# A hand-written order of every engine up to the third step of a software-pipelined attention and feed-forward kernel on one Trainium2 core

## The chip, the core and the metric

The kernel runs on one core of one Trainium2 chip. The metric is the device time of one execution in microseconds (us), lower is better. Five engines work side by side, each through its own list of instructions in order: PE (TensorE, matrix products), DVE (VectorE), ACT (ScalarE), POOL (GpSimd) and SP (SyncE, which here issues nearly all DMA transfers). They meet only at semaphores. An instruction that waits for a semaphore holds back everything behind it on its own engine.

## What is computed

The reference, cut to what matters (x is 32 x 128 x 1024, ctx is 32 x 128 x 256, the projections are 128 x 128, the dequantised weight is 1024 x 1024):

```python
def attend(up, down, Wq, Wk, Wv, Wskip):      # per batch element
    q, k, v = Wq @ up, Wk @ down, Wv @ down
    attention = softmax(q.T @ k / sqrt(128))  # 1024 x 256
    return Wskip @ up + (attention @ v.T).T
w = (unpacked_nibbles(qweight) - round(zeros / scales).T) * scales.T
x = x + attend(layernorm(x), ctx, Wq, Wk, Wv, Wskip)
x = x + layernorm(x) @ w + bias
```

## The kernel before

One batch element (a tile of 128 rows by 1024 columns) is one unit of work, and there are 32 of them. Below, f(b, j) is the function f for element b (from 0), part j. The pipeline is laid out over steps t: in step t the element b = t has its attention scores and probabilities made, n = t + 1 its first layernorm finished and its keys and values made, m = t + 2 its first statistics, a = t - 1 its attention output, residual and second layernorm, q = t - 2 its feed-forward product, and c = t - 3 its last output written. Each engine has a function step(t) with the order of its work in a step, and before it a function run_in() with a hand-written order for the first steps. In the kernel before, run_in covers steps 0 and 1 on every engine, and run_steps(step, 2) does the rest. There is no planner: the order on each engine is the order in the source, and the semaphores only hold an instruction back.

The work of one element, by engine, with the lines by which the profile knows it:

- PE. scores(b, j), j = 0 to 3: six products each into one of two banks (L891); the first needs keys_lo(b) of DVE, j = 0 and j = 2 need centred_lo(b, 0) and (b, 1) of POOL, j = 2 and 3 need exps(b, 0) and (b, 1) of ACT, and j = 0 and 1 need exps(b-1, 2) and (b-1, 3). keys_values(n) (L900, L902, L904) needs values_lo(n-1) and context_max(n) of DVE. skip_attend(a, h), h = 0, 1 (L917, L921), needs the transposed probabilities of the half, h. ffn(q, h) (L926, and L930 for ffn_terms, which adds bias and zero points out of seed_w): 17 products a half, from the transposed normalised rows xnt_hi and xnt_lo and the weight wf.
- DVE. stats1, aggregate1, variance1 (L594, L602, L608) for the first layernorm; value_scale(n) (L619 to L627), whose last instruction waits for inverse_std1(n) of POOL; keys_lo, values_lo (L645, L650, L652); row_max (L657); invert(b, j) (L662), the reciprocal of a row sum, after exps(b, j); probs_lo(b, h) (L666); residual(a, h) (L676); stats2, aggregate2 (L681 to L691); scale_product (L700); context_max (L614).
- ACT. centre, centred_hi (L433, L440), keys_hi, values_hi (L461 to L470), exps (L478), probs_hi(b, h) (L487), which needs two normalise of POOL, apply_norm2 and xn_high (L496, L505).
- POOL. normalise(b, j) (L255, two instructions), which waits for invert(b, j); inverse_std1(m) (L263); centred_lo(n, h) (L270); inverse_std2(a) (L277, L279); split_row_sum(a) (L289 to L295); xn_low(a) (L300, two instructions); write_out(c, h) (L249).
- SP. turn_probs(b, h): two DMA transposes, of the high and the low part of the probabilities; turn_xn(a): two DMA transposes, of xn_high and xn_low; loads of x and ctx; stores.

Some work is done once and lies within the run-in and step 2: nibbles(k) on DVE (L719, L720), k = 0 to 3, unpacks a quarter of the weight, and unpack(k) on ACT (L509, L510) turns it into wf, from which the first ffn(0, 0) waits quarter by quarter. zero_point_quotient, zero_point_remainder, zero_point_rounding and seed_sources on POOL (L315 to L358) are chains of small instructions, each of which waits for the one before; PE transposes their result (turn_seed_rows, L875) into bank y0, and DVE copies it to seed_w (seed_rows, L730). In the kernel before, ffn(0, 0) waits for seed_rows before it starts, since it writes the same bank y0.

Of the kernel before, what the change touches and what calls it, by code (L numbers as in the profile page):

```python
# [15 lines left out]
def xattn_ffn_program(nc, x, ctx_in, wq, wk, wv, wskip, qweight, scales, zeros, bias, out):  # L16
# [26 lines left out]
    with es:  # L43
# [100 lines left out]
        def _(sp):  # L144
# [84 lines left out]
        def _(pool):  # L229
# [106 lines left out]
            def zero_point_rounding():  # L336
# [24 lines left out]
            def run_in():  # L361
# [16 lines left out]
                inverse_std1(3)  # L378
# [35 lines left out]
            run_steps(step, 2)  # L414

        @block.scalar
        def _(act):
# [95 lines left out]
            def run_in():  # L513
# [22 lines left out]
                probs_hi(1, 0)  # L536
                exps(1, 3)
                unpack(1)
                keys_hi(2)
                values_hi(2)  # L540
                probs_hi(1, 1)
                apply_norm2(0)
                xn_high(0)

            def step(t):
# [11 lines left out]
                if t == 2:  # L557
                    unpack(2)
# [3 lines left out]
                if t == 2:  # L562
                    unpack(3)
# [10 lines left out]
            run_steps(step, 2)  # L574

        @block.vector
        def _(dve):
# [149 lines left out]
            def seed_rows():  # L727
# [69 lines left out]
            def step(t):
# [9 lines left out]
                if t == 2:  # L807
                    nibbles(3)
# [13 lines left out]
                if t == 2:  # L822
                    seed_rows()
# [29 lines left out]
            run_steps(step, 2)  # L853

        @block.tensor
        def _(pe):
# [109 lines left out]
            def run_in():  # L966
# [14 lines left out]
                skip_attend(0, 1)  # L981

            def step(t):
# [7 lines left out]
                if t == 2:  # L991
                    turn_seed_rows()
# [14 lines left out]
            run_steps(step, 2)  # L1007
# [24 lines left out]
```

## Time and profile before

| what | value |
|---|---|
| runs | 525.06, 525.08, 527.37 us (median 525.08) |
| the profiled execution | 525.56 us |
| its span in the trace | 523.6 us |
| busy share PE, DVE, ACT, POOL | 95%, 82%, 71%, 90% |
| chain that ended last | PE 82%, POOL 7%, DVE 4%, DMA 3%, ACT 2% |
| mean granted TensorE clock | 0.993 |

The profiled execution took 525.56 us, of which the trace spans 523.6. Times of instructions below are microseconds from the start of the span. Engines overlap, so the shares don't add up. The clock is given as a share of full speed (2.4 GHz is 1.00, 1.2 GHz is 0.50).

### The profile page before, as it was taken

To read this page: it belongs to the slowest core of one execution; us is meant where nothing else is said; L and a number is where in the kernel's file an instruction comes from. 1 tells how busy PE (TensorE), PEld (TensorE's weight loads), DVE (VectorE), ACT (ScalarE), POOL (GpSimd) and SP (SyncE) were. 2 spreads that over 40 slices of the span, in tenths; PEclk is the share of its full clock that TensorE was granted. 3 is DMA by queue.
4 is the path that set the end of the run, shared out by engine and by line. 5 is a ranking of instruction groups with operands and counts; after the bars stand their busy time and mean duration, and the time that the engine had idled before them with its cause. 6 is when DMAs were issued, how large, how long until landed. Compare 5 with 4: busy or idle time off the path is not lost.

```text
span 523.6 us, 9244 instructions
## 1 busy us (share of the span) xinstructions
PE 496.0 (95%) x2668; PEld 301.3 (58%) x2668; DVE 427.9 (82%) x981; ACT 373.0 (71%) x844; POOL 471.2 (90%) x717
## 2 busy tenths in 40 slices
PE   4638999999999999999999999999999999999996
PEld 3525565566666555666656566655656666565642
DVE  5899788889888888988888898888889888887752
ACT  3978877777877777787777778777776877777520
POOL 4899899999999999999999999999999999999753
PEclk9989999999999999999999999999999999999999
DMA  7537787797897789689788878988797799757753
GB/s 295 181 75 144 150 200 194 181 203 171 182 173 201 177 185 202 176 175 190 186 181 185 194 180 172 188 195 179 177 195 185 167 188 196 176 131 141 164 124 123
DMA packets 227059, 92.65 MB, mean 177 GB/s; under 512 B 209472, under 2 KB 214080, under 8 KB 227008
## 3 DMA queue, kind: packets, MB, share of 16 engines
q1 hardware_dynamic: 226288, 91.91, 77.4%
q8 instruction: 21, 0.34, 0.3%
q14 instruction: 30, 0.25, 0.2%
q10 hardware_dynamic: 720, 0.14, 0.1%
HBM read 23.87 MB, written 16.78 MB: 78 GB/s over the span
## 4 chain that ended last, share of the span: by engine, by line
PE 82%; POOL 7%; DVE 4%; DMA 3%; ACT 2%; issue 2%; SPq 1%; POOLq 0%; ACTq 0%
PE ps_y L926 39%; PE ps_e L891 15%; PE ps_o L921 13%; PE ps_o L917 7%; PE ps_kv L902 3%; PE ps_y L930 2%; PE ps_kv L904 2%; POOL sb_prob L255 2%; DMA sb_xnt_lo<-sb_xn_lo 1%; DMA sb_wskip<-in_L_xattn_Wskip_dram 1%; POOL sb_xc_lo L270 1%; ACT sb_prob L478 1%; POOL sb_xn_lo L300 1%; DVE sb_neg_max L657 1%; DVE sb_st L594 0%
## 5 line engine op out<-in xcount | busy, mean ns | idle before, releaser
L926 PE MATMUL ps_y<-sb_wf,sb_xnt_hi 128*128 128x512 f16 x512 | 191.9, 380 | 2.9 <-DMA sb_xnt_lo<-sb_xn_lo 1.8
L926 PE MATMUL ps_y<-sb_wf,sb_xnt_lo 128*128 128x512 f16 x512 | 191.8, 379 | 0.0
L478 ACT ACTIVATE sb_prob<-ps_e,sb_neg_max 128x256 f32<-128x256 f32 x256 | 118.5, 471 | 58.3 <-DVE sb_neg_max L657 58.3
L255 POOL TENSOR_SCALAR sb_prob<-sb_prob,sb_rsum 128x256 f32<-128x256 f32 x256 | 123.0, 494 | 14.9 <-DVE sb_rsum L662 14.8
L666 DVE TENSOR_TENSOR sb_p_lo<-sb_prob,sb_p_hi 128x1024 f16<-128x1024 f32 x64 | 78.1, 1220 | 49.2 <-ACT sb_p_hi L487 49.2
L891 PE MATMUL ps_e<-sb_k_hi,sb_xc_hi 128*128 128x256 f32 x256 | 90.2, 353 | 8.1 <-DVE sb_k_lo L645 5.6
L926 PEld LDWEIGHTS ps_y<-sb_wf,sb_xnt_hi 128*128 128x128 f16 x512 | 49.9, 98 | 62.5 <-DMA sb_xnt_lo<-sb_xn_lo 2.8
L249 POOL TENSOR_TENSOR sb_o<-sb_prod,sb_x 128x512 f32<-128x512 f32 x63 | 80.4, 1276 | 5.6 <-DVE sb_prod L700 5.5
L657 DVE TENSOR_REDUCE sb_neg_max<-ps_e 128x2 f32<-128x512 f32 x128 | 84.7, 681 | 0.4
L926 PEld LDWEIGHTS ps_y<-sb_wf,sb_xnt_lo 128*128 128x128 f16 x512 | 50.1, 98 | 56.6
L487 ACT ACTIVATE sb_p_hi<-sb_prob 128x1024 f16<-128x1024 f32 x64 | 67.3, 1052 | 18.5 <-issue 15.5
L270 POOL TENSOR_TENSOR sb_xc_lo<-sb_xc,sb_xc_hi 128x512 fp32r<-128x512 f32 x62 | 80.1, 1292 | 0.2 <-ACT sb_xc_hi L440 0.2
L496 ACT ACTIVATE sb_xn<-sb_x,sb_nb,sb_rstd 128x1024 f32<-128x1024 f32 x32 | 43.0, 1343 | 51.6 <-POOL sb_nb L279 51.6
L891 PE MATMUL ps_e<-sb_k_lo,sb_xc_hi 128*128 128x256 f32 x256 | 72.9, 285 | 0.0
L891 PE MATMUL ps_e<-sb_k_hi,sb_xc_lo 128*128 128x256 f32 x256 | 72.6, 284 | 0.0
L300 POOL TENSOR_TENSOR sb_xn_lo<-sb_xn,sb_xn_hi 128x512 f16<-128x512 f32 x63 | 72.5, 1172 | 0.1
L891 PEld LDWEIGHTS ps_e<-sb_k_hi,sb_xc_hi 128*128 128x128 f32 x256 | 49.2, 192 | 20.3 <-DVE sb_k_lo L645 6.5
L700 DVE TENSOR_TENSOR sb_prod<-ps_y,sb_scale_row 128x512 f32<-128x512 f32 x64 | 43.8, 684 | 12.9 <-PE ps_y L930 12.4
L478 ACT ACTIVATION_READ_ACCUMULATOR sb_prob<-ps_e,sb_neg_max 128x1 f32 x256 | 51.1, 200 | 0.0
L891 PEld LDWEIGHTS ps_e<-sb_k_lo,sb_xc_hi 128*128 128x128 f32 x256 | 49.4, 193 | 2.3
L676 DVE SCALAR_TENSOR_TENSOR sb_x<-ps_o,sb_o_scale,sb_x 128x512 f32<-128x512 f32 x64 | 47.2, 738 | 3.7 <-PE ps_o L921 3.7
L921 PE MATMUL ps_o<-sb_pt_hi,sb_v_hi 128*128 128x512 f16 x128 | 49.2, 384 | 0.5 <-DMA sb_pt_lo<-sb_p_lo 0.4
(123 smaller groups left out, 925.2 us busy)
## 6 DMA issues: line engine op xcount, KB each, us to landing
sb_x<-in_x_dram SPq DMA_DIRECT2D x32, 512.0 KB, 4.0
out_dram<-sb_o SPq DMA_DIRECT2D x64, 256.0 KB, 2.4
sb_ctx<-in_ctx_dram SPq DMA_DIRECT2D x32, 128.0 KB, 2.7
sb_q<-in_L_ffn_qweight_dram SPq DMA_DIRECT2D x4, 512.0 KB, 9.0
sb_pt_hi<-sb_p_hi SPq DMA_TRANSPOSE x64, 3.0
sb_pt_lo<-sb_p_lo SPq DMA_TRANSPOSE x64, 2.8
sb_scale_row<-in_L_ffn_scales_dram SPq DMA_DIRECT2D x1, 512.0 KB, 10.3
sb_xnt_hi<-sb_xn_hi SPq DMA_TRANSPOSE x32, 2.8
```

The source lines that it names most:

```text
L249: pool.tensor_tensor(o_sb[:, c % 2, cols], prod[:, h, :], x1[:, c % 3, cols], ALU.add).then_inc(out_done[h], 1)
L255: last = pool.tensor_scalar(prob[:, j, t, :], prob[:, j, t, :], rsum[:, j, t:t + 1], P_SCALE, ALU.mult, ALU.mult)
L270: pool.tensor_tensor(xc_lo[:, n % 3, cols], xc[:, cols], xc_hi[:, n % 3, cols].bitcast(F32), ALU.subtract).then_inc(xclo_done, 1)
L300: last = pool.tensor_tensor(xn_lo[:, k:k + KT // 2, :], xn[:, k:k + KT // 2, :], xn_hi[:, k:k + KT // 2, :], ALU.subtract)
L478: done = act.activation(prob[:, j, t, :], ps_e[j % 2][:, t, :], ACT.Exp, bias=neg_max[:, j, t:t + 1], accum_out=esum[:, j, t:t + 1])
L487: act.activation(p_hi[:, h, :, :].rearrange("n k (t m) -> n k t m", m=P), prob[:, 2 * h:2 * h + 2, :, :].rearrange("n j t (k m) -> n k (j ...
L657: dve.tensor_reduce(neg_max[:, j, :], ps_e[j % 2][:, :, :], AX.X, ALU.max, negate=True).then_inc(max_done[j], 1)
L666: dve.tensor_tensor(p_lo[:, h, :, :].rearrange("n k (t m) -> n k t m", m=P), prob[:, 2 * h:2 * h + 2, :, :].rearrange("n j t (k m) -> n k ...
L676: dve.scalar_tensor_tensor(x1[:, a % 3, cols], ps_o[h][:, :], o_scale[:, a % 3:a % 3 + 1], x_sb[:, a % 4, cols], ALU.mult, ALU.add).then_i ...
L891: last = pe.matmul(ps_e[j % 2][:, t, :], xc_p[s][:, b % 3, cols], k_p[m][:, b % 2, :], start=i == 0, stop=i == 2)
L921: last = pe.matmul(ps_o[h][:, :], v_p[s][:, a % 3, k * P:(k + 1) * P], pt_p[m][:, h, k, :], start=False, stop=k == MT - 1 and i == 2)
L926: pe.matmul(ps_y[h][:, :], xnt_p[s][:, q % 2, kt, :], wf[:, kt, h * HALF:(h + 1) * HALF], start=kt == 0 and s == 0, stop=False)
```

## The change

Run_in is extended on PE, DVE, ACT and POOL so that it covers step 2 as well, and run_steps begins with step 3 there; on SP run_in is reordered and run_steps still begins with step 2. What differs in order:

- DVE: after row_max(1, 3) stands value_scale(2), and keys_lo(2) comes ahead of nibbles(1), probs_lo(1, 0) and the statistics stats1(3), aggregate1(3), variance1(3); row_max(2, 0) comes ahead of probs_lo(1, 1). In what was step 2, nibbles(3) and seed_rows stand after row_max(2, 2); stats1(4), aggregate1(4), variance1(4), and invert(2, 2) with them, come after residual(1, 1), row_max(2, 3), stats2(1, 1) and aggregate2(1). keys_lo(n) waits for values_hi(n) for every n from 2 on.
- POOL: zero_point_rounding is cut after its sixth instruction, and its last four (zero_point_sign) come after inverse_std2(0); split_row_sum(0) and xn_low(0) come ahead of seed_sources; inverse_std1(3) comes after normalise(2, 0), behind seed_sources; inverse_std1(4) comes after normalise(2, 3).
- ACT: probs_hi(1, 0) comes after values_hi(2); unpack(1) after xn_high(0); unpack(2) ahead of centre(3); unpack(3) after exps(2, 2); exps(2, 3) ahead of probs_hi(2, 0).
- PE: keeps the order of step 2, but turn_seed_rows comes after skip_attend(1, 1) and writes bank y1, and ffn(0, 0) waits for seed_rows only before its last product.
- SP: turn_xn is cut in two; load_ctx(4) comes ahead of turn_probs(1, 0), and the high transpose of turn_xn(0) ahead of turn_probs(1, 1).

```diff
@@ SP
-            def turn_xn(a):
+            def turn_xn_hi(a):
...
+            def turn_xn_lo(a):
...
                 sp.wait_ge(kv_done, 2)
                 load_ctx(3)
-                turn_probs(1, 0)
                 sp.wait_ge(kv_done, 3)
                 load_ctx(4)
+                turn_probs(1, 0)
                 sp.wait_ge(x1_done[1], 1)
                 load_x(4)
+                turn_xn_hi(0)
                 turn_probs(1, 1)
-                turn_xn(0)
+                turn_xn_lo(0)
@@ POOL
                 zero_point_rounding()
-                inverse_std1(3)
                 normalise(1, 2)
                 normalise(1, 3)
                 inverse_std2(0)
-                seed_sources()
+                zero_point_sign()
                 split_row_sum(0)
                 xn_low(0)
+                seed_sources()
+                normalise(2, 0)
+                inverse_std1(3)
+                normalise(2, 1)
+                normalise(2, 2)
+                centred_lo(3, 0)
+                inverse_std2(1)
+                centred_lo(3, 1)
+                normalise(2, 3)
+                inverse_std1(4)
+                write_out(0, 0)
+                split_row_sum(1)
+                xn_low(1)
@@ ACT
                 exps(1, 2)
-                probs_hi(1, 0)
                 exps(1, 3)
-                unpack(1)
                 keys_hi(2)
                 values_hi(2)
+                probs_hi(1, 0)
                 probs_hi(1, 1)
                 apply_norm2(0)
                 xn_high(0)
+                unpack(1)
+                exps(2, 0)
+                unpack(2)
+                centre(3)
+                exps(2, 1)
+                keys_hi(3)
+                values_hi(3)
+                exps(2, 2)
+                unpack(3)
+                centred_hi(3)
+                exps(2, 3)
+                probs_hi(2, 0)
+                apply_norm2(1)
+                probs_hi(2, 1)
+                xn_high(1)
@@ DVE
             def keys_lo(n):
                 src = (ps_o[1], ps_y[0], ps_kv)[min(n, 2)]
-                if n == 2:
-                    dve.wait_ge(kvhi_done, 3)
+                if n >= 2:
+                    dve.wait_ge(kvhi_done, n + 1)
...
                 row_max(1, 3)
+                value_scale(2)
                 stats2(0, 0)
+                invert(1, 2)
+                residual(0, 1)
+                invert(1, 3)
+                stats2(0, 1)
+                aggregate2(0)
+                keys_lo(2)
                 nibbles(1)
-                invert(1, 2)
+                probs_lo(1, 0)
+                values_lo(2)
+                row_max(2, 0)
+                probs_lo(1, 1)
+                context_max(3)
+                nibbles(2)
                 stats1(3, 0)
                 stats1(3, 1)
                 aggregate1(3)
                 variance1(3)
-                value_scale(2)
-                residual(0, 1)
-                probs_lo(1, 0)
-                invert(1, 3)
-                stats2(0, 1)
-                aggregate2(0)
-                keys_lo(2)
-                values_lo(2)
-                context_max(3)
-                nibbles(2)
-                probs_lo(1, 1)
+                invert(2, 0)
+                residual(1, 0)
+                row_max(2, 1)
+                value_scale(3)
+                row_max(2, 2)
+                nibbles(3)
+                seed_rows()
+                invert(2, 1)
+                keys_lo(3)
+                values_lo(3)
+                stats2(1, 0)
+                residual(1, 1)
+                row_max(2, 3)
+                stats2(1, 1)
+                aggregate2(1)
+                invert(2, 2)
+                stats1(4, 0)
+                stats1(4, 1)
+                aggregate1(4)
+                invert(2, 3)
+                variance1(4)
+                probs_lo(2, 0)
+                context_max(4)
+                scale_product(0, 0)
+                probs_lo(2, 1)
@@ PE
             def ffn_terms(q, h):
+                if q == 0:
+                    pe.wait_ge(rows_done, 1)
...
             def ffn_ready(q, h):
                 if ran(q, 1):
                     pe.wait_ge(prod_done[h], q)
-                else:
+                elif h == 1:
                     pe.wait_ge(rows_done, 1)
...
+                scores(2, 0)
+                keys_values(3)
+                skip_attend(1, 0)
+                scores(2, 1)
+                scores(2, 2)
+                skip_attend(1, 1)
+                turn_seed_rows()
+                scores(2, 3)
+                ffn(0, 0)
+                ffn(0, 1)
```

The bank of turn_seed_rows and of the copy in seed_rows is `ps_y[1]` after the change, `ps_y[0]` before. The lines `if t == 2:` with their calls are gone from the four functions step(t).

## Rows read from the trace of the kernel before

**Rows 1.** Stretches: us; busy (count) of PE, PEld, DVE, ACT, POOL; clock; DMA share; GB/s

```profile
35.00:40.00 5.00, 2.27 (x9) 2.09 (x10) 4.93 (x13) 2.50 (x4) 4.89 (x8) 0.50 0.47 123
...
110.00:125.00 15.00, 15.00 (x83) 9.30 (x83) 12.77 (x31) 11.16 (x27) 14.16 (x21) 1.00 0.82 200
```

**Rows 2.** Waits of PE from 0 to 75 us: us in total, times, longest

```profile
PE ps_e L891 <- DVE sb_k_lo L645: 5.6, 2, 5.4
...
PE ps_y L926 <- DMA sb_xnt_lo<-sb_xn_lo: 1.1, 1, 1.1
PE ps_y L926 <- ACT sb_wf L510: 1.0, 1, 1.0
```

**Rows 3.** Busy time from 54 us on, columns as in rows 1

```profile
54.00:60.00 6.00, 6.00 (x34) 3.50 (x33) 4.33 (x7) 4.95 (x9) 4.68 (x7) 1.00 0.62 129
60.00:500.00 440.00, 439.87 (x2395) 267.57 (x2394) 371.95 (x853) 325.65 (x748) 413.82 (x607) 1.00 0.82 180
```

**Rows 4.** Timeline of PE: start, duration (us), engine, line, what [idle before it]

```profile
31.97 0.38 PE L921 MATMUL ps_o<-sb_pt_hi,sb_v_lo 128*128 128x512 f16 x1
37.73 0.58 PE L891 MATMUL ps_e<-sb_k_hi,sb_xc_hi 128*128 128x256 f32 x1 [5.38 <-DVE sb_k_lo L645]
...
39.18 0.23 PE L900 MATMUL ps_m<-sb_amax,sb_ones 128*128 128x1 bf16 x1
...
43.01 0.38 PE L921 MATMUL ps_o<-sb_pt_hi,sb_v_lo 128*128 128x512 f16 x1
...
49.98 0.39 PE L926 MATMUL ps_y<-sb_wf,sb_xnt_hi 128*128 128x512 f16 x1 [1.08 <-DMA sb_xnt_lo<-sb_xn_lo]
...
58.31 0.47 PE L891 MATMUL ps_e<-sb_k_hi,sb_xc_hi 128*128 128x256 f32 x1
...
66.40 0.39 PE L926 MATMUL ps_y<-sb_wf,sb_xnt_hi 128*128 128x512 f16 x1
```

**Rows 5.** Timeline of DVE

```profile
27.52 1.13 DVE L650 SCALAR_TENSOR_TENSOR sb_wsk_lo<-sb_proj,sb_sk_scale,sb_wsk_hi 128x128 fp32r<-128x128 f32 x1
...
30.76 0.71 DVE L719 TENSOR_SCALAR sb_nib<-sb_q 128x1024 int32<-128x1024 int32 x1
...
32.06 1.26 DVE L594 BATCH_NORM_STATS2 sb_st<-sb_x 128x6 f32<-128x512 f32 x2
...
34.95 1.22 DVE L666 TENSOR_TENSOR sb_p_lo<-sb_prob,sb_p_hi 128x1024 f16<-128x1024 f32 x1
...
37.19 0.48 DVE L645 SCALAR_TENSOR_TENSOR sb_k_lo<-ps_kv,sb_rstd,sb_k_hi 128x256 fp32r<-128x256 f32 x1
...
46.92 1.20 DVE L730 COPY sb_seed_w<-ps_y 16x1024 bf16<-16x1024 bf16 x1
...
52.58 0.15 DVE L691 TENSOR_SCALAR sb_ve<-sb_mv 128x1 f32<-128x1 f32 x1
```

**Rows 6.** Timeline of POOL

```profile
30.66 0.26 POOL L338 TENSOR_SCALAR sb_zp<-sb_zp 128x8 f32<-128x8 f32 x1
31.01 1.10 POOL L339 TENSOR_SCALAR sb_zp<-sb_zp 128x8 f32<-128x8 f32 x1
32.19 0.20 POOL L340 TENSOR_TENSOR sb_zp<-sb_zp 128x8 f32<-128x8 f32 x1
...
46.99 0.94 POOL L255 TENSOR_SCALAR sb_prob<-sb_prob,sb_rsum 128x256 f32<-128x256 f32 x2
47.89 0.57 POOL L263 TENSOR_TENSOR sb_rstd<-sb_ve,sb_neg_half 128x1 f32<-128x1 f32 x1
...
54.89 1.83 POOL L255 TENSOR_SCALAR sb_prob<-sb_prob,sb_rsum 128x256 f32<-128x256 f32 x2 [1.15 <-DVE sb_rsum L662]
56.92 1.27 POOL L249 TENSOR_TENSOR sb_o<-sb_prod,sb_x 128x512 f32<-128x512 f32 x1 [0.21 <-DVE sb_prod L700]
...
60.07 2.28 POOL L300 TENSOR_TENSOR sb_xn_lo<-sb_xn,sb_xn_hi 128x512 f16<-128x512 f32 x2
```

**Rows 7.** PE by stretch: us, busy (instructions), granted clock, DMA share, GB/s

```profile
34.50:35.00 0.50, 0.00 (x0) 0.52 0.00 0
41.00:41.50 0.50, 0.50 (x4) 0.65 2.82 277
```

More of the change, by code:

```diff
@@ L181, in turn_xn @@
                     last_hi_loaded if a == B - 1 else xnt_loaded[par], 16)
+            def turn_xn_lo(a):
+                par = a % 2
                 sp.wait_ge(rs_done, a + 1)
@@ L204, in step @@
                 if ran(a):
-                    turn_xn(a)
+                    turn_xn_hi(a)
+                    turn_xn_lo(a)
             def run_in():
@@ L343, in zero_point_rounding, with zero_point_sign @@
                 link(pool.tensor_scalar(size, size, ROUND, None, ALU.subtract))
+            def zero_point_sign():
+                size, sign, small = zp(WORK), zp(WORK + 1), zp(TMP)
                 link(pool.tensor_tensor(size, size, sign, ALU.mult))
@@ L413, in _ @@
             run_in()
-            run_steps(step, 2)
+            run_steps(step, 3)
         @block.scalar
@@ L556, in step @@
                     exps(b, 1)
-                if t == 2:
-                    unpack(2)
                 if ran(b):
@@ L561, in step @@
                     probs_hi(b, 0)
-                if t == 2:
-                    unpack(3)
                 if ran(b):
@@ L573, in _ @@
             run_in()
-            run_steps(step, 2)
+            run_steps(step, 3)
         @block.vector
@@ L730, in seed_rows @@
                 dve.tensor_copy(seed_w[0:ROWS, :].rearrange("m (p t) -> m p t", t=ZT),
-                                ps_y[0][0:ROWS, :].bitcast(BF16).rearrange("m (t p) -> m p t", p=P)).then_inc(rows_done, 1)
+                                ps_y[1][0:ROWS, :].bitcast(BF16).rearrange("m (t p) -> m p t", p=P)).then_inc(rows_done, 1)
             def run_in():
@@ L806, in step @@
                     value_scale(n)
-                if t == 2:
-                    nibbles(3)
                 if ran(m):
@@ L821, in step @@
                     row_max(b, 2)
-                if t == 2:
-                    seed_rows()
                 if ran(a):
@@ L852, in _ @@
             run_in()
-            run_steps(step, 2)
+            run_steps(step, 3)
         @block.tensor
@@ L874, in turn_seed_rows @@
                 for t in range(ZT):
-                    last = pe.transpose(ps_y[0][0:ROWS, :].bitcast(BF16)[:, t * P:(t + 1) * P], seed_src[:, t, :],
+                    last = pe.transpose(ps_y[1][0:ROWS, :].bitcast(BF16)[:, t * P:(t + 1) * P], seed_src[:, t, :],
                                         ident16[:, :])
@@ L990, in step @@
                     skip_attend(a, 0)
-                if t == 2:
-                    turn_seed_rows()
                 if ran(b):
@@ L1006, in _ @@
             run_in()
-            run_steps(step, 2)
+            run_steps(step, 3)
 _INS = ["x", "ctx_1024", "L0_xattn_Wq", "L0_xattn_Wk", "L0_xattn_Wv", "L0_xattn_Wskip",
```

## The prediction

> **What bounds the kernel now.** I read busy time by stretch first, then the waits, then the timelines of the first 80 us. From step 3 on the only limit is PE: 15.00 of 15.00 us busy, with POOL close behind at 14.16 [rows 1]. From 54 to 500 us PE was busy in 445.87 of 446 us [rows 3]. What lies in front of that is ragged: between 35 and 40 us PE was busy 2.27 of 5 us at half its clock [rows 1], because scores(2, 0) waited 5.4 us for keys_lo(2); later ffn(0, 0) waited 1.1 us for the transposed xn_low(0) and 1.0 us for the weight [rows 2]. So the change is worth what it moves the first moment from which PE no longer waits. I measure that at the start of ffn(1, 0), at 66.40 us before, with scores(3, 0) at 58.31 as the mark ahead of it [rows 4]. PE's work behind that is the same and full, so a shift there is a shift of the end.
>
> **Step 1: scores(2, 0), a gain of 3.0 us.** keys_lo(2) started at 37.19. Taken from in front of it are nibbles(1), stats1(3) with its two small ones and probs_lo(1, 0): slots of 1.2, 1.6 and 1.1 us by start-to-start, 3.9 in all [rows 5]. What stays then meets two waits: 0.2 us for keys_values(2), and 0.7 for the end of skip_attend(0, 1) at 32.35 [rows 4]. 37.2 - 3.9 + 0.9 = 34.2, and scores(2, 0) at 34.7, not 37.73.
>
> **Step 2: most of it is lost at keys_values(3).** It needs context_max(3), which now stands behind nibbles(1) 1.2, probs_lo(1, 0) 1.1, values_lo(2) 0.8, row_max(2, 0) 0.6 and probs_lo(1, 1) 1.1. 34.6 + 4.8 = 39.4, plus 0.5 for itself: 39.9 against 39.18 before [rows 4]. PE idles from 36.1. The clock had fallen to half at 34.5 and came back at about 41.3, some 3.6 us after PE resumed [rows 4, 7]; resuming at 39.9 I let it come back at 43.5, so keys_values(3) and skip_attend(1, 0) take 4.8 us, to 44.8 (before: to 43.4). Then scores(2, 1) and (2, 2), 1.4 us, and skip_attend(1, 1), 2.0, to 48.2 us; turn_seed_rows 0.5; scores(2, 3); ffn(0, 0) at 49.4. xn_low(0) is ready at 43.4 (step 3), so that wait of 1.1 us is gone. unpack(3) is done at 51.3, just ahead of the seventh pair at 52.0. The two ffn(0, h) took 58.31 - 49.98 less the 1.0 us wait, 7.35 [rows 2, 4]: PE is free at 56.8 us. If nothing else held, that would be 1.5 us gained.
>
> **Step 3: POOL reaches inverse_std1(3) late.** Between 30.66 and 47.89 POOL never idled: ten links of rounding, inverse_std1(3), three normalise, inverse_std2(0), seed_sources, split_row_sum(0), xn_low(0) [rows 6]. The new order does exactly these before the first standard deviation of element 3 is ready. The sum depends on holds: L339 took 1.10 us beside nibbles(1), its neighbour of the same size 0.20 [rows 5, 6], and the same is seen beside probs_lo. Four such holds stay (nibbles 1 and 2, both probs_lo), one, beside nibbles(3), goes, 0.8 us. 30.7 + 17.2 - 0.8 gives 47.1; I take 47.3. xn_low(0), now ahead of seed_sources, ends at 43.4 and not 47.0.
>
> By the Trainium skill (GPSIMD Engine Reference, Specifications) POOL's SBUF interfaces contend with Vector instructions that have two SBUF inputs, and the first of values_lo is one. If it held POOL too, its two calls would add about 0.6 us. The trace has the reverse there: L650 took 1.13 us while POOL's centred_lo ran on [rows 5], so I add nothing.
>
> **Step 4: DVE waits behind it.** value_scale(3) ends with an instruction that needs inverse_std1(3). Before, that was long done. Now DVE has run everything up to there by about 46.7 and waits to 47.3. Queued behind are row_max(2, 2), nibbles(3) and seed_rows, and only then invert(2, 1), for which POOL's normalise(2, 1) waits. 47.5 + 0.6 + 1.2 = 49.3 for seed_rows. From seed_rows to the end of aggregate2(1) the old trace shows 46.92 to 52.73, 5.8 us [rows 5], and it holds just what the new order puts ahead of invert(2, 2). So invert(2, 1) comes at 50.5 and invert(2, 2) at 55.1 (before: 50.30).
>
> **Step 5: POOL idles twice and is late for the rest.** From 46.99 to 62.35 POOL did normalise(2, 0) to xn_low(1): 15.4 us, of which 1.15 and 0.21 idle and 0.9 the first normalise, so 13.1 us of work, holds included [rows 6]. The new list has the same 13.1 us from normalise(2, 1) on. It starts at 50.6, stops from 51.5 to 55.1 for invert(2, 2), and ends at 50.6 + 13.1 + 3.6 = 67.3 us, 4.9 later than before.
>
> **Step 6: what PE sees.** The transpose of xn_low(0) let PE start 3.0 us after POOL was done (47.0 to 49.98) [rows 4, 6]. 67.3 + 3.0 = 70.3 for ffn(1, 0), 3.9 us after the 66.40 of before. A second chain ends close by: normalise(2, 3) is done at 61.5, probs_hi(2, 1) takes 1.0, probs_lo(2, 1) ends at 64.4 after waiting for POOL's write_out, and row_max(3, 0) stands behind it. The old probs_lo(2, 1) ended 7.1 us ahead of ffn(1, 0); keeping that whole gives 71.5, +5.1, but some of it was PE's own pace. Between 3.9 and 5.1 I take 4.3, nearer the first, whose terms are all durations. In step 4 POOL's next xn_low is ready at about 82, its transpose at 85, ffn(2, 0) due at 86: nothing is added, nothing recovered, since PE is full. The SP and ACT moves cost nothing: the transposes of element 1 land by 45 us and are read at 46.2; exps(2, 3) is done by 54.8 while POOL is what probs_hi waits for.
>
> Sum: 525.56 + 4.3 = 529.9 for a profiled execution like this one; the median of the runs is 0.5 below it, so **529.4 us**. 0.5% (2.6 us) is about what a measurement here can tell from no change.
>
> **Rivals.**
>
> *The early gain stays (faster).* The place is xn_low(1) on POOL. PE free at 56.8 is worth 1.5 us, 523.5 in all, if xn_low(1) is done by 56.8 + 8.1 - 3.0 = 61.9 us. For it: PE's own path through step 2 has no new wait, and a clock that stayed up would add up to 0.8. Against it: it needs POOL 5.4 us earlier than I have it, and with no wait on DVE at all invert(2, 2) comes at about 51, so xn_low(1) at 64. It would take holds on POOL much shorter than the traces show. A gain over 2.6 us is 0.05, one up to there 0.05.
>
> *The delay is smaller (within 0.5%).* The holds overlap more, inverse_std1(3) is ready at 46, DVE hardly waits, POOL's second stop is 2 us: ffn(1, 0) at 68, +1.6, 526.7. Chance 0.14.
>
> *The clock falls again.* On the forecast PE idles about 4 us between scores(3, 1) and scores(3, 2), waiting for exps(3, 0). Before, 2.2 us without work from 32.35 was followed by half clock at 34.5, which lasted until 41.3 [rows 4, 7]. A fall here puts scores(3, 2), skip_attend(2, 1) and scores(3, 3), 3.4 us at full speed, partly at half: +1 to +2 us, 530.4 to 531.4. The Trainium skill (TensorE: Matmul & The Clock Gate, What's actually happening) says that the throttled state is the default and activity lifts it, so a busier start would keep the clock and a new hole lose it. Chance 0.26.
>
> The forecast itself, +2.6 to +5.2, has 0.50. In all: slower 0.76, within 0.5% 0.19, faster 0.05. The range is 526.2 to 531.6: from the smaller delay to the clock case.
>
> **What would show it.** Right: scores(2, 0) at 34.7; keys_values(3) near 40; the last instruction of value_scale(3) waiting for L263 near 47; POOL idle twice for 3 us before L255, put down to invert; xn_low(1) ending near 67; waits of PE before scores(3, 2) and ffn(1, 0); 15.25 us steps from there. Wrong: L263 of element 3 ready before 45, or POOL without those stops, or PE that catches up later.

## The result and the profile after

The changed kernel took 530.62 us (median of 5 runs, 529.74 to 531.53) against 525.09 us for the kernel before in the same runs: ratio 1.0105, 95% interval [1.0092, 1.0119], 5.5 us slower. The forecast was 529.4 us. The profiled execution took 530.62 us, its span is 528.7 us (before: 525.56 and 523.6).

Three views of the changed kernel answer to the rows of before. First its waits, of PE from 0 to 80 us, then of POOL and DVE from 28 to 75 us (us in total, times, longest). Lines have moved: L943 is scores, L952 the first product of keys_values, L973 the attention, L978 the feed-forward product, L260 normalise, L268 inverse_std1, L275 centred_lo, L282 inverse_std2, L305 xn_low, L498 exps, L507 probs_hi, L644 context_max, L657 the last instruction of value_scale, L675 keys_lo, L692 invert, L696 probs_lo, L706 residual, L721 the last of aggregate2.

```profile
PE ps_e L943 <- ACT sb_prob L498: 4.5, 3, 3.2
PE ps_m L952 <- DVE sb_amax L644: 4.1, 1, 4.1
PE ps_e L943 <- DVE sb_k_lo L675: 2.7, 2, 2.4
...
POOL sb_prob L260 <- DVE sb_rsum L692: 6.5, 2, 3.4
...
DVE sb_x L706 <- PE ps_o L973: 2.7, 2, 2.1
DVE sb_sk_scale L657 <- POOL sb_rstd L268: 0.9, 1, 0.9
```

The wait for keys_lo(2), 5.4 us long before [rows 2, 4], is 2.4 us. In its place PE waits 4.1 us for context_max(3), and 3.2 us for exps(3, 0). POOL, which never idled at this point before, waits 6.5 us in two stops for invert.

The timelines of PE, DVE and POOL, in this order (start, duration, engine, line, what, [idle before it]):

```profile
34.46 0.39 PE L943 MATMUL ps_e<-sb_k_hi,sb_xc_hi 128*128 128x256 f32 x1 [2.42 <-DVE sb_k_lo L675]
...
39.56 0.16 PE L952 MATMUL ps_m<-sb_amax,sb_ones 128*128 128x1 bf16 x1 [4.12 <-DVE sb_amax L644]
...
56.71 0.36 PE L943 MATMUL ps_e<-sb_k_hi,sb_xc_hi 128*128 128x256 f32 x1
...
65.87 0.36 PE L943 MATMUL ps_e<-sb_k_hi,sb_xc_hi 128*128 128x256 f32 x1 [3.21 <-ACT sb_prob L498]
...
68.09 0.63 PE L973 MATMUL ps_o<-sb_pt_lo,sb_v_hi 128*128 128x512 f16 x1
...
71.04 0.39 PE L978 MATMUL ps_y<-sb_wf,sb_xnt_hi 128*128 128x512 f16 x1
```

```profile
47.09 0.21 DVE L657 TENSOR_SCALAR sb_sk_scale<-sb_v_scale,sb_rstd 128x1 f32<-128x1 f32 x1 [0.89 <-POOL sb_rstd L268]
...
50.15 0.14 DVE L692 RECIPROCAL sb_rsum<-sb_esum 128x2 f32<-128x2 f32 x1
...
54.20 0.15 DVE L692 RECIPROCAL sb_rsum<-sb_esum 128x2 f32<-128x2 f32 x1
...
61.80 1.67 DVE L696 TENSOR_TENSOR sb_p_lo<-sb_prob,sb_p_hi 128x1024 f16<-128x1024 f32 x1 [3.18 <-ACT sb_p_hi L507]
```

```profile
46.41 0.57 POOL L268 TENSOR_TENSOR sb_rstd<-sb_ve,sb_neg_half 128x1 f32<-128x1 f32 x1
50.39 0.96 POOL L260 TENSOR_SCALAR sb_prob<-sb_prob,sb_rsum 128x256 f32<-128x256 f32 x2 [3.41 <-DVE sb_rsum L692]
54.45 0.94 POOL L260 TENSOR_SCALAR sb_prob<-sb_prob,sb_rsum 128x256 f32<-128x256 f32 x2 [3.09 <-DVE sb_rsum L692]
...
64.27 2.27 POOL L305 TENSOR_TENSOR sb_xn_lo<-sb_xn,sb_xn_hi 128x512 f16<-128x512 f32 x2
```

And PE by stretches (us, busy (instructions), granted clock, DMA share, GB/s):

```profile
34.00:35.00 1.00, 0.54 (x4) 1.00 0.58 134
35.00:36.00 1.00, 0.43 (x4) 1.00 0.58 128
36.00:38.00 2.00, 0.00 (x0) 0.57 0.01 3
...
67.00:68.00 1.00, 1.00 (x4) 0.50 0.28 64
68.00:69.00 1.00, 1.00 (x4) 0.50 1.29 114
69.00:70.00 1.00, 1.00 (x5) 0.50 0.83 197
70.00:71.00 1.00, 1.00 (x7) 0.79 1.05 401
```

**Where the time went.** scores(3, 0) starts at 56.71 us, 1.6 earlier than the 58.31 of before [rows 4]: the change does bring PE out of step 2 earlier. Then PE stands still for 0.47, 0.51 and 3.21 us inside step 3, and its clock falls to half from 67 to a little past 70 us, with products of 0.63 us where they take 0.38. ffn(1, 0) starts at 71.04, 4.64 later than the 66.40 of before. 4.64 + 1.6 = 6.24 us are lost in step 3. Of these 4.60 lie ahead of skip_attend(2, 1), which starts at 66.66 (before: 63.66): the three stops are 4.19 of them, and the other 0.41 goes with the stops too, because back to back the products start 0.12 to 0.22 us apart though each lasts 0.28 to 0.38, so that a stop costs more than its idle time. The last 1.64 go with the half clock: from skip_attend(2, 1) to ffn(1, 0) PE takes 4.38 us for what took 2.74. From ffn(1, 0) to ffn(30, 0) the old trace takes 438.21 us (66.40 to 504.61), the new one 438.83 (71.04 to 509.87), and the rest of the span is 0.16 shorter: 4.64 + 0.62 - 0.16 = 5.10, the difference of the spans.

### The profile page after: what moved, and what is told of

Read it like the earlier page. It is cut to its first block, busy times and chain, and to the rows that moved or that the text cites. A ratio compares the mean times of both kernels' runs of the same rounds, so it can differ in the third digit from the quotient of the medians.

```text
span 528.7 us, 9242 instructions
## 1 busy us (share of the span) xinstructions
PE 497.9 (94%) x2636; PEld 302.6 (57%) x2668; DVE 428.8 (81%) x981; ACT 373.4 (71%) x844; POOL 470.3 (89%) x717
## 4 chain that ended last, share of the span: by engine, by line
PE 79%; POOL 7%; DVE 5%; issue 3%; DMA 3%; ACT 2%; SPq 1%; another core or an unknown queue 0%; POOLq 0%; ACTq 0%; DVEq 0%
PE ps_y L978 39%; PE ps_e L943 14%; PE ps_o L973 13%; PE ps_o L969 7%; PE ps_kv L954 3%; PE ps_kv L956 2%; POOL sb_prob L260 2%; DMA sb_xnt_lo<-sb_xn_lo 2%; PE ps_y L984 1%; POOL sb_xc_lo L275 1%; DMA sb_wskip<-in_L_xattn_Wskip_dram 1%; DVE sb_neg_max L687 1%; POOL sb_xn_lo L305 1%; ACT sb_prob L498 1%; POOL sb_rstd L282 1%
## 5 line engine op out<-in xcount | busy, mean ns | idle before, releaser
L978 PE MATMUL ps_y<-sb_wf,sb_xnt_hi 128*128 128x512 f16 x512 | 191.9, 380 | 3.8 <-DMA sb_xnt_lo<-sb_xn_lo 2.2
L978 PE MATMUL ps_y<-sb_wf,sb_xnt_lo 128*128 128x512 f16 x512 | 191.8, 379 | 0.0
L498 ACT ACTIVATE sb_prob<-ps_e,sb_neg_max 128x256 f32<-128x256 f32 x256 | 118.5, 471 | 60.5 <-DVE sb_neg_max L687 60.5
L260 POOL TENSOR_SCALAR sb_prob<-sb_prob,sb_rsum 128x256 f32<-128x256 f32 x256 | 121.6, 489 | 20.7 <-DVE sb_rsum L692 20.6
L696 DVE TENSOR_TENSOR sb_p_lo<-sb_prob,sb_p_hi 128x1024 f16<-128x1024 f32 x64 | 79.0, 1234 | 51.0 <-ACT sb_p_hi L507 51.0
L943 PE MATMUL ps_e<-sb_k_hi,sb_xc_hi 128*128 128x256 f32 x256 | 90.5, 353 | 8.9 <-ACT sb_prob L498 4.5
L978 PEld LDWEIGHTS ps_y<-sb_wf,sb_xnt_hi 128*128 128x128 f16 x512 | 50.0, 98 | 61.0 <-DMA sb_xnt_lo<-sb_xn_lo 2.9
L978 PEld LDWEIGHTS ps_y<-sb_wf,sb_xnt_lo 128*128 128x128 f16 x512 | 50.1, 98 | 56.8
L275 POOL TENSOR_TENSOR sb_xc_lo<-sb_xc,sb_xc_hi 128x512 fp32r<-128x512 f32 x62 | 80.1, 1292 | 0.1
L507 ACT ACTIVATE sb_p_hi<-sb_prob 128x1024 f16<-128x1024 f32 x64 | 67.2, 1050 | 16.3 <-issue 14.8
L943 PE MATMUL ps_e<-sb_k_lo,sb_xc_hi 128*128 128x256 f32 x256 | 72.8, 285 | 0.0
L943 PE MATMUL ps_e<-sb_k_hi,sb_xc_lo 128*128 128x256 f32 x256 | 72.5, 283 | 0.0
L305 POOL TENSOR_TENSOR sb_xn_lo<-sb_xn,sb_xn_hi 128x512 f16<-128x512 f32 x63 | 72.0, 1165 | 0.1
L943 PEld LDWEIGHTS ps_e<-sb_k_hi,sb_xc_hi 128*128 128x128 f32 x256 | 49.4, 193 | 21.9 <-issue 7.0
L706 DVE SCALAR_TENSOR_TENSOR sb_x<-ps_o,sb_o_scale,sb_x 128x512 f32<-128x512 f32 x64 | 47.3, 739 | 6.3 <-PE ps_o L973 6.1
L498 ACT ACTIVATION_READ_ACCUMULATOR sb_prob<-ps_e,sb_neg_max 128x1 f32 x256 | 51.1, 200 | 0.0
L943 PEld LDWEIGHTS ps_e<-sb_k_lo,sb_xc_hi 128*128 128x128 f32 x256 | 49.5, 193 | 2.3
L973 PE MATMUL ps_o<-sb_pt_hi,sb_v_hi 128*128 128x512 f16 x128 | 50.4, 393 | 0.5 <-DMA sb_pt_lo<-sb_p_lo 0.5
```

Source lines behind the costliest of these rows:

```text
L260: last = pool.tensor_scalar(prob[:, j, t, :], prob[:, j, t, :], rsum[:, j, t:t + 1], P_SCALE, ALU.mult, ALU.mult)
L275: pool.tensor_tensor(xc_lo[:, n % 3, cols], xc[:, cols], xc_hi[:, n % 3, cols].bitcast(F32), ALU.subtract).then_inc(xclo_done, 1)
L305: last = pool.tensor_tensor(xn_lo[:, k:k + KT // 2, :], xn[:, k:k + KT // 2, :], xn_hi[:, k:k + KT // 2, :], ALU.subtract)
L498: done = act.activation(prob[:, j, t, :], ps_e[j % 2][:, t, :], ACT.Exp, bias=neg_max[:, j, t:t + 1], accum_out=esum[:, j, t:t + 1])
L507: act.activation(p_hi[:, h, :, :].rearrange("n k (t m) -> n k t m", m=P), prob[:, 2 * h:2 * h + 2, :, :].rearrange("n j t (k m) -> n k (j ...
L696: dve.tensor_tensor(p_lo[:, h, :, :].rearrange("n k (t m) -> n k t m", m=P), prob[:, 2 * h:2 * h + 2, :, :].rearrange("n j t (k m) -> n k ...
```

## The experiments

Each kernel was measured beside the kernel before on one chip; chips and runs differ by some tenths, so the differences are taken from the median of before beside it.

| kernel | median us | before | difference | ratio, 95% interval |
|---|---|---|---|---|
| the changed kernel | 530.62 | 525.09 | +5.5 | 1.0105 [1.0092, 1.0119] |
| e1_inv22 | 527.19 | 525.33 | +1.9 | 1.0040 [1.0029, 1.0051] |
| e2_std3 | 529.54 | 525.33 | +4.2 | 1.0082 [1.0062, 1.0102] |
| e3_warm | 528.84 | 525.33 | +3.5 | 1.0063 [1.0048, 1.0078] |
| e4_first | 528.25 | 525.33 | +2.9 | 1.0050 [1.0030, 1.0069] |
| e5_inv21 | 527.75 | 524.95 | +2.8 | 1.0048 [1.0033, 1.0064] |
| e6_hi3 | 527.71 | 524.95 | +2.8 | 1.0049 [1.0035, 1.0064] |
| e7_ctx | 530.09 | 524.95 | +5.1 | 1.0094 [1.0076, 1.0111] |
| e8_all | 526.28 | 524.95 | +1.3 | 1.0023 [1.0013, 1.0033] |
| e9_more | 524.02 | 524.86 | -0.8 | 0.9985 [0.9976, 0.9994] |
| e10_cutpool | 529.90 | 524.86 | +5.0 | 1.0094 [1.0080, 1.0108] |

**e1_inv22: one reciprocal, earlier.**

```diff
@@ DVE, step 2
                 values_lo(3)
+                invert(2, 2)
                 stats2(1, 0)
...
                 aggregate2(1)
-                invert(2, 2)
```

> One move in the changed kernel: invert(2, 2) on DVE comes right after values_lo(3), ahead of stats2(1, 0), residual(1, 1), row_max(2, 3), stats2(1, 1) and aggregate2(1). My theory (POOL late because its normalise(2, 2) waits for this reciprocal): POOL's second stop of 3.1 us is all but gone, xn_low(1) ends near 63.5 in place of 66.5 us, scores(3, 2) waits some 3 us less, the clock stays up, ffn(1, 0) starts at 66.5 to 67 in place of 71.04: about 4.2 us faster, 526.4. Rival (POOL has slack, and the hole in PE is made by the clock and PE's own order): within 0.7 us of the changed kernel, 530.6.

Measured: +1.9 in place of +5.5 us, so one instruction of 0.15 us, moved up past six others, is worth 3.7 us with all that follows from it (1.86 against 5.53). The timeline of POOL, and behind it the stretches of PE:

```profile
49.98 0.96 POOL L260 TENSOR_SCALAR sb_prob<-sb_prob,sb_rsum 128x256 f32<-128x256 f32 x2 [3.41 <-DVE sb_rsum L692]
51.15 0.93 POOL L260 TENSOR_SCALAR sb_prob<-sb_prob,sb_rsum 128x256 f32<-128x256 f32 x2 [0.21 <-DVE sb_rsum L692]
54.00 0.55 POOL L282 TENSOR_TENSOR sb_rstd<-sb_ve,sb_neg_half 128x1 f32<-128x1 f32 x1 [0.69 <-DVE sb_ve L721]
...
61.67 2.28 POOL L305 TENSOR_TENSOR sb_xn_lo<-sb_xn,sb_xn_hi 128x512 f16<-128x512 f32 x2
```

```profile
60.00:66.00 6.00, 4.89 (x27) 1.00 0.86 156
66.00:70.00 4.00, 3.52 (x19) 1.00 0.67 205
```

The second stop is 0.21 us in place of 3.09; 0.69 us of it comes back at the next input, aggregate2(1). xn_low(1) starts 2.6 us earlier than in the changed kernel, the clock stays at 1.00, and ffn(1, 0) starts at 67.70. The first 30 us of executions differ by some tenths, so I count from the start of scores(2, 0): ffn(1, 0) comes after 33.6 us in place of 36.6. I estimate that about 1.0 of these 3.0 us is the clock that stayed up (worked out under e3_warm, from e2_std3 and e7_ctx) and the other 2.0 the place of the reciprocal. My theory holds; the rival, that POOL has slack here, is out.

**e2_std3: the wait of DVE for POOL taken away.**

```diff
@@ POOL
                 xn_low(0)
+                inverse_std1(3)
                 seed_sources()
                 normalise(2, 0)
-                inverse_std1(3)
```

> One move in the changed kernel: inverse_std1(3) on POOL comes ahead of seed_sources. My theory: DVE's wait of 0.9 us in value_scale(3) goes, both reciprocals come 0.9 us earlier, and so does everything behind them: 0.9 us faster, 529.7, with POOL still stopping twice, 2.5 and 3 us. Rival (this wait is the root of the whole loss, as the order of steps 3 and 4 of the prediction could be read): 4 us faster or more, 526.5.

Measured: +4.2, a gain of 1.3 us. The waits of POOL and DVE, 28 to 75 us:

```profile
POOL sb_prob L260 <- DVE sb_rsum L692: 6.3, 2, 3.2
...
DVE sb_seed_w L760 <- PE ps_y L927: 0.4, 1, 0.4
```

DVE's wait in value_scale(3) is gone from the list, but 0.4 us of it come back in seed_rows, which now waits for PE, and POOL still stops twice, for 6.3 us. Counted from scores(2, 0), xn_low(1) ends after 31.9 us, in the changed kernel after 32.1. So the late standard deviation is a small term, 0.2 us on POOL, and the place of the two reciprocals the large one. ffn(1, 0) comes 1.0 us earlier than in the changed kernel all the same, because the clock didn't fall behind PE's long hole. The line of PE that ends this hole, and the stretch around it (the changed kernel has 0.81 in the same stretch):

```profile
66.14 0.35 PE L943 MATMUL ps_e<-sb_k_hi,sb_xc_hi 128*128 128x256 f32 x1 [3.22 <-ACT sb_prob L498]
```

```profile
62.00:70.00 8.00, 4.32 (x25) 1.00 0.74 137
```

**e3_warm: the clock by itself.** 28 products that nothing uses fill PE's longest hole.

```diff
@@ PE, scores(b, j)
+                if b == 3 and j == 2:
+                    pe.wait_ge(prod_done[0], 1)
+                    for _ in range(28):
+                        pe.matmul(ps_y[0][:, 0:M], ones[:, :], seed_w[:, 0:M], start=True, stop=True)
                 if j >= 2:
                     pe.wait_ge(exp_done[j - 2], b + 1)
```

> The changed kernel with 28 products of 128x256, written to bank y0 and used by nothing, put in front of scores(3, 2), where PE waits 3.2 us for exps(3, 0). They take 3.0 us of that hole at full clock. Theory A (the fall of the clock at 67 us costs PE, but ffn(1, 0) can't start before the transpose of xn_low(1) lands, near 69.7): granted clock stays 1.00 from 60 to 75 us, 1.2 us faster, 529.4. Theory B (the clock costs all of the half-speed time): 2 us faster, 528.6. Theory C (the clock is not what delays ffn(1, 0)): no change, 530.6.

Measured: +3.5, a gain of 2.0 us, with the hole as long as before but filled. The stretch of PE and three lines of its timeline (four lines of source are added, so scores is L947 here and the feed-forward product L982):

```profile
62.00:70.00 8.00, 7.44 (x54) 1.00 0.80 195
```

```profile
62.25 3.23 PE L939 MATMUL ps_y<-sb_seed_w,sb_ones 128*128 128x256 bf16 x28
...
69.02 0.38 PE L947 MATMUL ps_e<-sb_k_hi,sb_xc_hi 128*128 128x256 f32 x1 [0.52 <-ACT sb_prob L498]
69.84 0.39 PE L982 MATMUL ps_y<-sb_wf,sb_xnt_hi 128*128 128x512 f16 x1
```

The clock stays at 1.00. But this doesn't show that the useless products kept it there: in the profiles of e2_std3 and e7_ctx the hole is as long (3.22 and 3.19 us) and empty, and the clock stays at 1.00 behind it too. From the start of scores(2, 0) to ffn(1, 0) the changed kernel takes 36.6 us, this one 35.6, and e2_std3 and e7_ctx take 35.6 as well. So in the profiles a clock that stays up is worth 1.0 us, filled hole or not: of the 1.64 us a wait of 0.52 for exps(3, 1), with what goes with a stop, takes the rest. That is nearer theory A's size, though no wait for the transpose is shown in front of ffn(1, 0). The medians give 2.0, theory B's size. The spans differ by 1.9 us (526.8 against 528.7): 1.0 of it up to here, 0.2 in the start, and 0.6 is a wait in mid-run that the changed kernel has and this one hasn't (see the last section). What the filling by itself is worth stays open.

**e4_first: the early part with the old step 2.** The order up to the end of step 1 is the changed one, with inverse_std1(3) ahead of seed_sources; step 2 of DVE, ACT and POOL is the general step, with nibbles(3) behind value_scale(3), seed_rows behind row_max(2, 2), unpack(2) and unpack(3) as before the change.

> The first part of the change alone: the orders of all engines up to the end of step 1 as changed (with inverse_std1(3) ahead of seed_sources), then step 2 on DVE, ACT and POOL in the order of the general step as before, where invert(2, 2) stands ahead of residual(1, 1); PE as changed. My theory (the loss lies in the new step 2 alone): the early gain is given back by value_scale(3) waiting at the head of step 2, but no more than that: xn_low(1) ends near 63, ffn(1, 0) at 66 to 67, 525 to 526. Rival (the early reordering itself makes POOL late): 529 or more.

Measured: +2.9, outside of both: neither 525 to 526 nor 529 and more. One line of PE's timeline shows what I had not counted (L935 is the feed-forward product here, L519 unpack):

```profile
54.41 0.39 PE L935 MATMUL ps_y<-sb_wf,sb_xnt_hi 128*128 128x512 f16 x1 [2.46 <-ACT sb_wf L519]
```

ffn(0, 0) starts at 49.19 in place of 49.98, and with that the old place of unpack(3) is too late: 2.5 us of wait for the last quarter of the weight, and then a granted clock of 0.50 from 56 to 58 us. xn_low(1) starts at 60.73 us there, so on POOL the theory is borne out. The early part alone gains nothing without its own step 2.

**e5_inv21 and e6_hi3: two more waits in front of POOL.**

```diff
@@ DVE, e5 and e6, on top of e1
                 row_max(2, 2)
+                invert(2, 1)
                 nibbles(3)
                 seed_rows()
-                invert(2, 1)
+                invert(2, 2)
                 keys_lo(3)
                 values_lo(3)
-                invert(2, 2)
@@ ACT, e6 only
                 exps(2, 2)
-                unpack(3)
                 centred_hi(3)
+                unpack(3)
```

> The kernel of e1_inv22, and also invert(2, 1) ahead of nibbles(3) and invert(2, 2) right behind seed_rows, so that POOL's first stop of 3.4 us shrinks to about 1 us. My theory (a stop is worth only what the next late input leaves): centred_lo(3, 0) needs centred_hi(3) of ACT, which ends at 51.7 behind unpack(3), and inverse_std2(1) needs aggregate2(1) at 54.0 as in e1_inv22, so POOL's idle time moves there and little is won: 526.9 against 527.2. Rival (POOL's idle time adds up, each us of stop taken away is a us gained): 524.7.

> The kernel of e5_inv21, and also centred_hi(3) ahead of unpack(3) on ACT. My theory: centred_lo(3, 0) comes 1.3 us earlier, but inverse_std2(1), next on POOL, still waits for aggregate2(1) at about 54.0, so nothing more is won: 526.8. Rival (centred_hi(3) was the limit of e5_inv21): 1 us or more below e5_inv21.

Measured: +2.8 and +2.8, so neither wins anything over e1_inv22; they are 0.9 worse, with intervals of the ratio that overlap. POOL's waits, e5_inv21 first, then e6_hi3:

```profile
POOL sb_prob L260 <- DVE sb_rsum L692: 2.0, 2, 1.2
POOL sb_xc_lo L275 <- ACT sb_xc_hi L460: 1.0, 1, 1.0
POOL sb_rstd L282 <- DVE sb_ve L721: 0.8, 1, 0.8
```

```profile
POOL sb_rstd L282 <- DVE sb_ve L721: 1.8, 1, 1.8
POOL sb_prob L260 <- DVE sb_rsum L692: 1.7, 2, 1.1
```

The stop moves as expected: from invert(2, 1) to centred_hi(3), and from there to aggregate2(1). The rival, that each microsecond of stop is a microsecond of gain, is out. In the profiles only e5_inv21 is behind: from scores(2, 0) to ffn(1, 0) e1_inv22 takes 33.6 us, e5_inv21 34.2 and e6_hi3 33.6. The clock differs in both. In e1_inv22 scores(2, 0) still ran at full clock and the clock was back for 42 to 43 us; in e5_inv21 it fell while scores(2, 0) ran and came back near 45. The same stretches, e1_inv22 and then e5_inv21:

```profile
34.00:35.00 1.00, 0.93 (x6) 1.00 1.08 247
...
42.00:43.00 1.00, 1.00 (x6) 1.00 0.35 71
```

```profile
34.00:35.00 1.00, 0.76 (x5) 0.80 0.85 195
...
44.00:45.00 1.00, 1.00 (x5) 0.58 1.28 287
```

With it residual(1, 0) of DVE waits 3.03 us for PE in e5_inv21, 1.73 in e1_inv22. Nothing ahead of that point differs between the two programs, so the moment of the fall changes from one execution to another. Whether the clock, the chip or chance makes up the 0.9 us in the medians isn't settled.

**e7_ctx: PE's wait of 4.1 us taken away.**

```diff
@@ DVE
                 keys_lo(2)
+                values_lo(2)
+                context_max(3)
                 nibbles(1)
                 probs_lo(1, 0)
-                values_lo(2)
                 row_max(2, 0)
                 probs_lo(1, 1)
-                context_max(3)
```

> One move in the changed kernel: values_lo(2) and context_max(3) on DVE come right after keys_lo(2), so that keys_values(3) starts near 35.5 us in place of 39.56 and PE's wait of 4.1 us for context_max(3) is gone or moves to the transposed probabilities. My theory (POOL decides, and nothing on POOL comes earlier, since value_scale(3) waits for it): within 0.7 us of the changed kernel, 530.6, and scores(2, 0) to ffn(0, 1) 0 to 2 us earlier with the time lost again before scores(3, 2). Rival (step 2 of the prediction, the loss at keys_values(3), reaches the end): 2 to 4 us faster, 527 to 528.6.

Measured: +5.1, within 0.4 us of the changed kernel. Waits of PE:

```profile
PE ps_o L973 <- DMA sb_pt_lo<-sb_p_lo: 4.8, 3, 3.2
PE ps_e L943 <- ACT sb_prob L498: 3.6, 2, 3.2
```

keys_values(3) starts at 34.95 us, the wait becomes one of 3.2 us for the transposed probabilities, POOL's stops are the same 6.5 us, and xn_low(1) ends 32.1 us after the start of scores(2, 0) in both kernels. What PE loses in step 2 doesn't reach the end, because POOL decides. The hole of step 3 is there as before, but the clock stays up behind it:

```profile
65.31 0.36 PE L943 MATMUL ps_e<-sb_k_hi,sb_xc_hi 128*128 128x256 f32 x1 [3.19 <-ACT sb_prob L498]
```

```profile
62.00:70.00 8.00, 4.35 (x25) 1.00 0.80 171
```

So a hole of 3.2 us is followed by half clock in the profile of the changed kernel and by full clock in those of e7_ctx and e2_std3. In e10_cutpool, below, the hole is 2.7 us and the clock falls (0.50 from 64 to 67 us). What decides it these runs don't show.

**e10_cutpool: which chain reaches ffn(1, 0).**

```diff
@@ POOL
                 normalise(2, 3)
-                inverse_std1(4)
-                write_out(0, 0)
                 split_row_sum(1)
                 xn_low(1)
+                inverse_std1(4)
+                write_out(0, 0)
```

> One move in the changed kernel: inverse_std1(4) and write_out(0, 0), 1.8 us of POOL's work, come behind xn_low(1) in place of ahead of it; DVE, ACT and PE as changed. If the transpose of xn_low(1) is what ffn(1, 0) waits for (the first chain of step 6 of the prediction): 1 to 1.8 us faster, 529. If the second chain decides (normalise(2, 3), probs_hi(2, 1), probs_lo(2, 1), row_max(3, 0), exps(3, 0), then scores(3, 2) and skip_attend(2, 1) at half clock), as the trace of the changed kernel suggests: within 0.6 us of it, 530.3, since probs_lo(2, 1) only loses its short wait for write_out(0, 0).

Measured: +5.0, 0.5 us less than the changed kernel, with the wait for exps(3, 0) at 2.7 in place of 3.2. xn_low(1) ends at 64.29 us in place of 66.54, and nothing follows from it. In the changed kernel itself the transposed xn_low(1) lands at 70.0 us (issued at 66.61, 3.4 us to landing), 1.0 ahead of ffn(1, 0). So there ffn(1, 0) is reached last by the second chain, through normalise(2, 3), probs_lo(2, 1), row_max(3, 0) and exps(3, 0), not by the transpose of xn_low(1).

**e8_all and e9_more: a version that beats both.** e8_all joins e2, e6 and e7, with invert(2, 3) right after aggregate2(1) and centred_lo(3, 1) ahead of inverse_std2(1). e9_more adds to it:

```diff
@@ DVE
+                probs_lo(1, 0)
                 nibbles(1)
-                probs_lo(1, 0)
...
                 nibbles(3)
+                invert(2, 2)
+                stats2(1, 0)
                 seed_rows()
-                invert(2, 2)
                 keys_lo(3)
                 values_lo(3)
-                stats2(1, 0)
@@ POOL
                 normalise(2, 3)
-                inverse_std1(4)
-                write_out(0, 0)
                 split_row_sum(1)
                 xn_low(1)
+                inverse_std1(4)
+                write_out(0, 0)
@@ SP
-                turn_xn_hi(0)
                 turn_probs(1, 1)
+                turn_xn_hi(0)
```

> All moves together: e6_hi3, e7_ctx, inverse_std1(3) ahead of seed_sources, and for the end of step 2 invert(2, 3) right after aggregate2(1) on DVE and centred_lo(3, 1) ahead of inverse_std2(1) on POOL. My theory: POOL stops for less than 2 us in all after seed_sources, xn_low(1) ends near 61, PE leaves ffn(0, 1) near 55.5 and ffn(1, 0) starts at 63.6 to 64.5: 2 to 3 us faster than the kernel before, 522.6. Rival (something else of the new step 2, the weights through ACT or the transposes, takes its place): no faster than before, 525 or more.

> The kernel of e8_all, and also: on DVE probs_lo(1, 0) ahead of nibbles(1), and invert(2, 2) and stats2(1, 0) ahead of seed_rows; on SP turn_probs(1, 1) ahead of the high transpose of turn_xn(0); on POOL inverse_std1(4) and write_out(0, 0) behind xn_low(1). My theory: the waits of PE for transposed probabilities (4.6 us in e8_all) fall to 2 or 3, aggregate2(1) ends near 53.2, xn_low(1) near 61 in place of 63.1, ffn(1, 0) starts at 64 to 64.5: 1.5 to 2.5 us faster than the kernel before, 523. Rival (POOL's work up to xn_low(1) is all that counts and it is the same as before): 525, no gain.

e8_all: +1.3, as its rival had it; PE waits 4.6 us for transposed probabilities. seed_rows waits 1.05 us for PE, and invert(2, 2) behind it stops POOL for 1.25. e9_more: -0.8, ratio 0.9985 with an interval that ends below 1, smaller than the 1.5 to 2.5 us that I expected. Its lines of PE, then of POOL:

```profile
43.99 0.39 PE L973 MATMUL ps_o<-sb_pt_hi,sb_v_hi 128*128 128x512 f16 x1 [1.43 <-DMA sb_pt_lo<-sb_p_lo]
...
63.51 0.39 PE L943 MATMUL ps_e<-sb_k_hi,sb_xc_hi 128*128 128x256 f32 x1 [1.27 <-ACT sb_prob L498]
...
64.39 0.39 PE L978 MATMUL ps_y<-sb_wf,sb_xnt_hi 128*128 128x512 f16 x1
```

```profile
54.06 0.48 POOL L294 CAST sb_xn_lo<-sb_rs 128x3 bf16<-128x3 f32 x1 [0.64 <-ACT sb_xn L516]
55.97 2.73 POOL L305 TENSOR_TENSOR sb_xn_lo<-sb_xn,sb_xn_hi 128x512 f16<-128x512 f32 x2 [0.62 <-ACT sb_xn_hi L525]
```

POOL no longer stops for invert, and ffn(1, 0) starts at 64.39 us, 2.0 earlier than in the kernel before. In the profiles the spans differ by 1.6 us (522.0 against 523.6). The new order of run_in is thus not wrong as such: a version of it with the small outputs where other engines need them is a little faster than the old one. The two reciprocals alone don't do it (e6_hi3 is still 2.8 us slower than before), and what each of the further moves is worth wasn't tried one by one.

## Why the prediction was right, point by point

It was right in direction and in mechanism up to xn_low(1), 529.4 us predicted for 530.62 measured, within the range. Which chain reaches PE last it had wrong (step 6).

- Step 1, scores(2, 0) at 34.7: 34.46, with a wait of 2.4 us. Right.
- Step 2, keys_values(3) at 39.9 for want of context_max(3), and PE free at 56.8: 39.56, and scores(3, 0) at 56.71. Right. The clock fell at 36 us, after scores(2, 0), and not at 34.5 as I took over from the old trace; it was back at 43 as assumed. In the profiles of the other reordered kernels that wait here in the same way it falls between 33 and 37 us. e7_ctx shows that this loss is beside the point, which the step's heading didn't say.
- Step 3, inverse_std1(3) ready at 47.3: 46.98, and xn_low(0) done at 43.2 for 43.4. The four holds are there.
- Step 4, DVE waits for it to 47.3, then invert(2, 1) at 50.5 and invert(2, 2) at 55.1: the wait ends at 47.09, the reciprocals come at 50.15 and 54.20. The last is 0.9 early. Of that 0.35 is there already at invert(2, 1), and another 0.35 comes from the old stretch of 5.8 us: it held a values_lo whose first instruction took 0.75 us beside POOL, 0.40 in the new one. In the medians e2_std3, without the wait for POOL, gains 1.3 us (0.2 on POOL in its profile, the rest clock), and e1_inv22, with invert(2, 2) ahead of five other pieces of work, 3.7 us. The prediction named both, but put the wait first.
- Step 5, two stops of POOL and xn_low(1) done at 67.3: stops of 3.41 and 3.09 us, done at 66.54. Right, 0.8 early, as the step before.
- Step 6, the sum of +4.3: this term failed in its reasoning, though its size came out near. I leaned on the first chain, through the transpose of xn_low(1). e10_cutpool shows that the second one decides. The prediction had put this chain at +5.1 by keeping a distance of 7.1 us from the end of probs_lo(2, 1) to ffn(1, 0); it is 7.6. The 4.64 us of the profile are 1.6 us gained, 4.60 us lost with the three stops and 1.64 us of half clock. "Nothing is added" behind ffn(1, 0) was wrong by 0.6 us: 0.5 of it is a wait of 0.60 near 437 us, where the old trace has none, and 0.1 lies between there and ffn(30, 0), where PE waits 1.57 us for the last transposes and the old trace has 0.71 and 0.40.
- The rival of the clock, given 0.26, came true in the profiled execution: the clock fell behind the hole I had named, and that cost 1.64 us, within its +1 to +2; its total of 530.4 to 531.4 holds the median. It doesn't come true in every execution. The five runs of the changed kernel have a mean granted clock of 0.983 in the three slower ones (530.62, 531.36, 531.53 us) and of 0.987 in the two faster (529.74, 529.83); in the trace the fall in step 3 takes 0.003 off the mean. So I estimate that the clock fell there in three of the five, but only one of them was traced. Where it stayed up, the forecast of 529.4 is 0.4 us off. The Trainium skill (TensorE: Matmul & The Clock Gate, What's actually happening) says that activity lifts the throttle. The traces agree in part: the clock is 0.50 from 67 to 70 us behind the hole of the changed kernel and 1.00 from 62 to 70 where e3_warm fills it, but also 1.00 behind the same empty hole in e2_std3 and e7_ctx.
- The rival of the early gain is refused in the changed kernel by POOL's stops, as it said it would be. Its claim that it needs POOL much earlier is borne out by e9_more, where the stops for invert are gone and a gain remains. One number in it is wrong: that invert(2, 2) comes at about 51 with no wait on DVE. By step 4 the wait is only 0.6 us, and in e2_std3, where it is gone, invert(2, 2) comes at 54.45.

## What to carry to other kernels

When an order is written by hand for an engine that others wait for, list for each of its small outputs who needs it and how full that engine is: here a reciprocal of 0.15 us placed behind 2.9 us of longer work stopped an engine that is 94% busy in steady state. Its place was worth 3.7 us in the medians, while all the large pieces that the change had moved brought PE to step 3 only 1.6 us earlier. Taking away a wait that isn't the last one moves the idle time to the next late input (e5, e6, e7); chase the chain until the bounding engine itself starts earlier. A hole in TensorE's work can be paid again in half clock behind it, here with 1.6 us after a hole of 3.2 us, but two other executions had the same hole and kept the clock. Give it a price and a chance in the sum, and compare several executions before you credit an edit with the difference.

## What was not expected

- The clock behind a hole of 3.2 us: half in the profile of the changed kernel, full in those of e2_std3 and e7_ctx, whose programs differ from it only before the hole. Filling the hole with products that nothing uses gained 2.0 us in the medians (e3_warm); how much of that is the filling isn't shown.
- The profiles of all the reordered kernels but e3_warm have one wait of 0.5 to 0.6 us for the transpose of xn_low in mid-run, between 430 and 437 us; the kernel before and e3_warm have none. At ffn(30, 0) the reordered kernels wait 0.8 to 1.6 us, the kernel before 0.71. The instructions there are in the same order in all; what is new is that keys_lo waits for values_hi in every step, and e3_warm has that too. This took back part of e9_more's gain; what causes it wasn't tried.
